# A strided convolution moved wholly onto TensorE, in 16 tiles of 32 x 32

## What is computed

```python
# 512 channels in, 256 out: each output channel has two input channels, a 3 x 3 window and stride 2
x = jax.lax.conv_general_dilated(sx, w_down, window_strides=(2, 2), padding=((1, 1), (1, 1)),
                                 feature_group_count=c2, dimension_numbers=('NCHW', 'OIHW', 'NCHW'))
# -> (8, 256, 64, 64)
labels = _kmeans_labels(xs)              # channels of image 0 into 8 clusters
v5 = ...                                 # cluster means of all images; then a small mixture fit
pre_up = gate[:, :, None, None] * x + x
up = jnp.repeat(pre_up, 2, axis=1) * w_up[None, :, None, None]
sx = _bilinear_up_x2(up) + sx            # end of layer 0
# layer 1: bias, resampling by 2 up, leaky relu, resampling by 2 down, with 12-tap filters
```

## Time and profile before

| | |
|---|---|
| median of 3 runs | 8536.89 us |
| the profiled execution | 8535.32 us |
| its span, first to last instruction | 8533.3 us |
| TensorE busy (matmuls; weight loads) | 92%; 81% |
| VectorE, ScalarE, GpSimd busy | 83%, 50%, 30% |
| granted TensorE clock, mean | 0.962 |
| DMA | 925.43 MB, mean 108 GB/s |
| convolution's work | about 37 to 1080 us |

### The profile page before, as it was taken

The page is one execution under the profiler, slowest core; times in us unless marked ns, Lnnn a source line. Parts: engine busy times, 40 slices in busy tenths (PEclk is TensorE's granted clock), DMA queues, the critical chain, the costliest instruction groups (busy, mean ns, idle before and its releaser), DMA issues.

```text
span 8533.3 us, 384310 instructions
## 1 busy us (share of the span) xinstructions
PE 7892.4 (92%) x151493; PEld 6882.4 (81%) x151493; DVE 7050.4 (83%) x12643; ACT 4274.0 (50%) x9070; POOL 2567.4 (30%) x3076
## 2 busy tenths in 40 slices
PE   7888855099999999999999999999999999999999
PEld 3444431089999999999999999999999999999999
DVE  8999933878888888888888888888888888888888
ACT  0000003356665556665556665566666556666555
POOL 0000000033333333333333333333333333333333
PEclk9999967599999999999999999999999999999999
DMA  7777713022222222222222222222222222222222
GB/s 294 297 292 292 296 61 129 0 82 84 84 84 84 84 84 84 84 84 84 84 84 84 84 84 84 84 84 84 84 84 84 84 84 84 84 84 84 84 84 81
DMA packets 1253329, 925.43 MB, mean 108 GB/s; under 512 B 175312, under 2 KB 1224912, under 8 KB 1234384
## 3 DMA queue, kind: packets, MB, share of 16 engines
q1 hardware_dynamic: 703248, 621.60, 21.5%
q10 hardware_dynamic: 550016, 303.11, 12.0%
HBM read 621.50 MB, written 303.04 MB: 108 GB/s over the span
## 4 chain that ended last, share of the span: by engine, by line
PE 80%; issue 0%; POOL 0%; DVE 0%; ACT 0%; DMA 0%; DVEq 0%; POOLq 0%
PE bank L976 37%; PE bank L965 20%; PE twin L965 15%; PE bank L970 4%; PE bank L1005 2%; PE twin L970 1%; DMA low<-conv_dram 0%; DVE leaky L1112 0%; ACT slope_t L1059 0%; POOL lift L946 0%; POOL low_f L943 0%; POOL img L931 0%; ACT res L1072 0%; DVE up L1105 0%; DVEq L810 0%
## 5 line engine op out<-in xcount | busy, mean ns | idle before, releaser
L1059 ACT ACTIVATE slope_t<-bank 128x512 f32<-128x512 f32 x4096 | 2223.2, 595 | 2263.2 <-PE bank L970 2263.2
L1112 DVE SCALAR_TENSOR_TENSOR leaky<-bank,slope_t 128x512 f32<-128x512 f32 x4096 | 2629.6, 683 | 781.4 <-ACT slope_t L1059 781.4
L970 PE MATMUL bank<-up_t,up 64*128 64x133 f32 x16384 | 2724.0, 286 | 0.0
L965 PE MATMUL bank<-up_t,up 64*128 64x133 f32 x16384 | 2672.1, 283 | 0.1
L976 PE MATMUL bank<-down_t,leaky 128*64 128x67 f32 x65536 | 2364.4, 225 | 0.7 <-DVE leaky L1112 0.5
L976 PEld LDWEIGHTS bank<-down_t,leaky 128*64 128x64 f32 x65536 | 2077.7, 137 | 259.5 <-DVE leaky L1112 1.0
L965 PEld LDWEIGHTS bank<-up_t,up 64*128 64x128 f32 x16384 | 2150.5, 187 | 52.3 <-PE bank L970 0.3
L970 PEld LDWEIGHTS bank<-up_t,up 64*128 64x128 f32 x16384 | 2147.7, 186 | 0.0
L1097 DVE SCALAR_TENSOR_TENSOR x_sum<-lift,coef,img 128x128 f32<-128x128 f32 x4096 | 1975.0, 522 | 8.8 <-POOL img L931 8.8
L931 POOL TENSOR_TENSOR img<-img,bias_all 128x512 f32<-128x512 f32 x1024 | 1089.7, 1064 | 2902.5 <-DMA img<-in_x 2902.5
L970 PE MATMUL twin<-up_t,x_sum 64*128 64x133 f32 x8192 | 1849.9, 306 | 0.0
(11 more groups left out here) (157 smaller groups left out, 3614.3 us busy)
## 6 DMA issues: line engine op xcount, KB each, us to landing
img<-in_x SPq DMA_DIRECT2D x1024, 256.0 KB, 2.8
out<-res ACTq DMA_DIRECT2D x1024, 256.0 KB, 2.2
rows_in<-in_x SPq DMA_DIRECT2D x48, 4224.0 KB, 13.9
rows_in<-in_x SPq DMA_DIRECT2D x16, 4096.0 KB, 13.7
conv_dram<-conv ACTq DMA_DIRECT2D x64, 512.0 KB, 4.1
xb<-conv_dram SPq DMA_DIRECT2D x8, 4096.0 KB, 13.4
low<-conv_dram SPq DMA_DIRECT2D x512, 64.0 KB, 2.5
xx<-conv_dram SPq DMA_DIRECT2D x2, 2048.0 KB, 10.0
```

Source lines behind the costliest of these rows:

```text
L965: return pe.matmul(acc[:, 0:UP_REACH], src, up_t[0:HALF, 0:UP_REACH], start=first, stop=False, skip_group_check=True)
L970: return pe.matmul(acc[:, UH - UP_REACH:UH], src, up_t[HALF:P, UH - UP_REACH:UH], start=first, stop=False, skip_group_check=True)
L1059: nc.scalar.activation(slope_t[i][:], u2_acc[1 - p][i][:], ACT.Copy, scale=SLOPE * GAIN).then_inc(slope_out, 1)
L1112: v.scalar_tensor_tensor(out=leaky[1 - m % 2][:, i].rearrange("p k w -> p (k w)"), in0=u2_acc[1 - m % 2][i][:], scalar=GAIN, in1=slope_t[i ...
```

## The change

All 16 output rows of a unit are made on TensorE. The array is used as 16 tiles of 32 x 32. Tile (rt, c) has as its stationary operand the diagonal of the 32 channels 32 rt to 32 rt + 31, reads those channels' partitions, and writes to PSUM partitions 32 c to 32 c + 31 of bank 4 (n % 2) + rt: the row tile chooses the channels and the bank, and the column tile chooses which four of the 16 output rows are made. So one tap is 16 matmuls of 4 x 64 = 256 columns. The result lies in PSUM as (row group c, channel within rt) on the partitions and rt over the banks; ScalarE copies four banks into `conv`, and stores it with four DMAs, one for each c, whose pieces are 1 KB (four rows of one channel).

VectorE's passes, `v_done` and `vec_step` go; `diag` shrinks to a 32-wide diagonal for each tap. TensorE's stream has no loop any more: it is written out for all 64 units. The other engines keep their loops.

```diff
-V_ROWS = 10
-T_ROWS = QR - V_ROWS
+T = 32
+NT = P // T
+T_ROWS = QR // NT
...
+    parts["eyes"] = np.tile(np.eye(T, dtype=np.float32), (NT, 1))
...
-                diag = sb("diag", [P, CB * TAPS, P])
+
+                diag = sb("diag", [P, CB * TAPS, T])
                 rows_in = [sb(f"rows_in{i}", [P, 2, IN_ROWS, W]) for i in range(2)]
-                conv = [sb(f"conv{i}", [P, QR, WO]) for i in range(2)]
+                conv = [sb(f"conv{i}", [P, NT, T_ROWS * WO]) for i in range(2)]
...
-                def conv_in(n, i, kh, kw, r0, r1):
+                def conv_in(n, i, kh, kw, rt, r0, r1):
 
                     c0 = (1, 0, 1)[kw]
-                    return rows_in[n % 2][:, i, 2 * r0 + kh:2 * (r1 - 1) + kh + 1:2, c0:c0 + 2 * (63 if kw == 0 else 64) - 1:2]
+                    return rows_in[n % 2][T * rt:T * (rt + 1), i, 2 * r0 + kh:2 * (r1 - 1) + kh + 1:2,
+                                          c0:c0 + 2 * (63 if kw == 0 else 64) - 1:2]
...
                         if wait is not None:
-
-                            sp.wait_ge(v_done, wait)
                             sp.wait_ge(t_done, wait)
...
-                    v.tensor_tensor(diag[:], ident[:, None, :].to_broadcast([P, CB * TAPS, P]),
-                                    tap_w[:].rearrange("p b t -> p (b t)")[:, :, None].to_broadcast([P, CB * TAPS, P]),
+                    v.tensor_tensor(diag[:], const("eyes")[:, None, :].to_broadcast([P, CB * TAPS, T]),
+                                    tap_w[:].rearrange("p b t -> p (b t)")[:, :, None].to_broadcast([P, CB * TAPS, T]),
                                     ALU.mult).then_inc(diag_ready, 1)
...
-                    def unit(b, n, first):
-                        cb, q = n // NQ, n % NQ
-                        v.wait_ge(in_loaded[n % 2], 16 * (n // 2 + 1) if first else (16 * (UB // 2)) * b + 16 * (n // 2 + 1))
-                        if not (first and n < 2):
-
-                            v.wait_ge(conv_stored[n % 2], 16 * (n // 2) if first else (16 * (UB // 2)) * b + 16 * (n // 2))
-                        for s, (i, kh, kw) in enumerate(order):
-                            r0 = 1 if (q == 0 and kh == 0) else 0
-                            dst = conv[n % 2][:, r0:V_ROWS, (1 if kw == 0 else 0):]
-                            w = tap_w[:, cb, (i * 3 + kh) * 3 + kw:(i * 3 + kh) * 3 + kw + 1]
-                            src = conv_in(n, i, kh, kw, r0, V_ROWS)
-                            last = s == TAPS - 1
-                            if s == 0:
-                                ins = v.tensor_scalar(dst, src, w, None, ALU.mult)
-                            else:
-
-                                v.wait_ge(vec_step, (TAPS - 1) * n + s if first else (TAPS - 1) * UB * b + ((TAPS - 1) * n + s))
-                                ins = v.scalar_tensor_tensor(out=dst, in0=src, scalar=w, in1=dst, op0=ALU.mult, op1=ALU.add)
-                            ins.then_inc(v_done if last else vec_step, 1)
-
-                    for n in range(UB):
-                        unit(0, n, True)
-                    with v.Fori(1, B) as b:
-                        for n in range(UB):
-                            unit(b, n, False)
-
                 @block.tensor
...
 
-                    def unit(b, n, first):
-                        cb = n // NQ
-                        pe.wait_ge(in_loaded[n % 2], 16 * (n // 2 + 1) if first else (16 * (UB // 2)) * b + 16 * (n // 2 + 1))
-                        if not (first and n < 2):
-
-                            pe.wait_ge(t_copied, n - 1 if first else UB * b + (n - 1))
-                        acc = bank[n % 2][:, 0:T_ROWS * WO].rearrange("p (r w) -> p r w", r=T_ROWS)
+                    def unit(b, n):
+                        cb, q = n // NQ, n % NQ
+                        g = UB * b + n
+                        pe.wait_ge(in_loaded[n % 2], 16 * (g // 2 + 1))
+                        if g >= 2:
+                            pe.wait_ge(t_copied, g - 1)
                         for s, (i, kh, kw) in enumerate(order):
-                            mm = pe.matmul(acc[:, :, (1 if kw == 0 else 0):],
-                                           diag[:, cb * TAPS + (i * 3 + kh) * 3 + kw, :],
-                                           conv_in(n, i, kh, kw, V_ROWS, QR), start=(s == 0), stop=(s == TAPS - 1),
-                                           skip_group_check=True)
+
+                            for c in range(NT):
+                                r0 = 1 if (q == 0 and c == 0 and kh == 0) else 0
+                                for rt in range(NT):
+                                    acc = bank[4 * (n % 2) + rt][T * c:T * (c + 1), 0:T_ROWS * WO].rearrange("p (r w) -> p r w", r=T_ROWS)
+                                    mm = pe.matmul(acc[:, r0:, (1 if kw == 0 else 0):],
+                                                   diag[T * rt:T * (rt + 1), cb * TAPS + (i * 3 + kh) * 3 + kw, :],
+                                                   conv_in(n, i, kh, kw, rt, T_ROWS * c + r0, T_ROWS * (c + 1)),
+                                                   start=(s == 0), stop=(s == TAPS - 1), skip_group_check=True)
                         mm.then_inc(t_done, 1)
 
-                    for n in range(UB):
-                        unit(0, n, True)
-                    with pe.Fori(1, B) as b:
+                    for b in range(B):
                         for n in range(UB):
-                            unit(b, n, False)
+                            unit(b, n)
 
                 @block.scalar
                 def _(act):
@@ -271,15 +247,17 @@
                         cb, q = n // NQ, n % NQ
                         act.wait_ge(t_done, n + 1 if first else UB * b + (n + 1))
                         if not (first and n < 2):
-                            act.wait_ge(conv_stored[n % 2], 16 * (n // 2) if first else (16 * (UB // 2)) * b + 16 * (n // 2))
-                        nc.scalar.activation(conv[n % 2][:, V_ROWS:, :].rearrange("p r w -> p (r w)"),
-                                             bank[n % 2][:, 0:T_ROWS * WO], ACT.Copy).then_inc(t_copied, 1)
+                            act.wait_ge(conv_stored[n % 2], 16 * NT * (n // 2) if first else (16 * NT * (UB // 2)) * b + 16 * NT * (n // 2))
+                        for rt in range(NT):
+                            ins = nc.scalar.activation(conv[n % 2][:, rt, :], bank[4 * (n % 2) + rt][:, 0:T_ROWS * WO], ACT.Copy)
+                        ins.then_inc(t_copied, 1)
 
                         act.wait_ge(t_copied, n + 1 if first else UB * b + (n + 1))
-                        act.wait_ge(v_done, n + 1 if first else UB * b + (n + 1))
                         rows = conv_dram[cb * P:(cb + 1) * P] if first else conv_dram[bass.ds(C * b + cb * P, P)]
-                        act.dma_start(rows[:, q * QR * WO:(q + 1) * QR * WO],
-                                      conv[n % 2][:].rearrange("p r w -> p (r w)")).then_inc(conv_stored[n % 2], 16)
+                        rows = rows.rearrange("(t c) p -> c t p", t=NT)
+                        for c in range(NT):
+                            at = (q * QR + c * T_ROWS) * WO
+                            act.dma_start(rows[:, :, at:at + T_ROWS * WO], conv[n % 2][T * c:T * (c + 1)]).then_inc(conv_stored[n % 2], 16)
 
                     for n in range(UB):
                         unit(0, n, True)
@@ -287,7 +265,7 @@
                         for n in range(UB):
                             unit(b, n, False)
                     for i in range(2):
-                        act.wait_ge(conv_stored[i], 16 * B * UB // 2)
+                        act.wait_ge(conv_stored[i], 16 * NT * B * UB // 2)
 
 
         def clusters(soh, sohn):
```

More of the change, by code:

```diff
@@ L142, in convolution @@
                 tap_w = sb("tap_w", [P, CB, TAPS])
-                diag = sb("diag", [P, CB * TAPS, P])
+                diag = sb("diag", [P, CB * TAPS, T])
                 rows_in = [sb(f"rows_in{i}", [P, 2, IN_ROWS, W]) for i in range(2)]
-                conv = [sb(f"conv{i}", [P, QR, WO]) for i in range(2)]
+                conv = [sb(f"conv{i}", [P, NT, T_ROWS * WO]) for i in range(2)]
                 in_loaded = [sem(f"in_loaded{i}") for i in range(2)]
                 conv_stored = [sem(f"conv_stored{i}") for i in range(2)]
-                vec_step = sem("vec_step")
                 diag_ready = sem("diag_ready")
-                v_done = sem("v_done")
                 t_done = sem("t_done")
```

## The result

The changed kernel takes 8902.34 us, the median of four runs (8897.23 to 8905.46), against 8536.72 before: a ratio of 1.0428, interval 1.041 to 1.0446. It is slower by 4.3%, 366 us; 8595 was forecast. The profiled execution took 8901.62 us. First the page of after: TensorE's and VectorE's slices and the granted clock, and the queue of instructions.

The account below looks back on a forecast made before the run. One DMA engine carrying data and instruction fetches was taken to bound the convolution: 37.1 us first load + 63 periods of 17.3 us (1090) + 15 = 1142 us, +60 us, forecast 8595 us; range 8250 to 9000.

Parts of the forecast that it names:

- the sum's own +60 us: Next stage's load after the convolution goes out at 1142 us instead of 1082.5, so the kernel is 60 us slower.
- VectorE sets the period before, and its passes are gone: Convolution: VectorE set the 16.3 us unit period; its taps, 952.2 us in 1088 passes, all on the path, go.
- The count of fetches: TensorE's written-out convolution: 1152 records a unit at 265 per 16 KB packet of q8 need 4.3 packets.
- It is not free for the load: Convolution loads: a fetch packet holds one DMA engine 0.94 to 1.23 us, so the load beside it lands later.
- That engine's work per unit would be 12.0 + 4.3 x 1.23 = 17.3 us: Convolution: one DMA engine carries data and all fetches and bounds the load, 17.3 us a unit; chance 0.45.
- fetches come too slowly: Rival, convolution: packets 5.5 us apart starve TensorE, 23.7 us a unit, 8999 us; chance 0.13.
- TensorE's 8.3 us a unit: Convolution matmuls: all sixteen tiles stream at once, 18 x 2 x 0.230 us = 8.3 us a unit.
- The two rivals that doubted this: Convolution: tiles don't all overlap (9598 us, chance 0.12); weight loads hold back same-row matmuls (9600 us or above, chance 0.05).
- ScalarE and its stores: Convolution: four evictions and four store issues take 3.4 us of a 17.3 us unit, beside the rest.

Follow-up runs that it names:

- the loop: The changed kernel with TensorE's unit looped, one body per block of channels, rows_in split by input channel, PSUM single: 8477.65 us, ratio 0.9932.

## Why the prediction was wrong

The sign, slower, was right and the size was not: +58 us forecast (the sum's own +60 us would make 8597, not 8595), +366 measured. As the step that was to give the sign failed, the sign is partly luck. Step by step:

- *VectorE sets the period before, and its passes are gone:* right. The beginning is the same, 37.1 and 37.2 us, and the resampling does not change: all of the difference is in the convolution.
- *The count of fetches*, 4.3 packets a unit: nearly; bursts of 128 matmuls with 128 weight loads give 4.5. 64 x 4.3 = 275 packets were forecast, and 288 came. The 265 records per packet were counted in a trace window and are 256.
- *"It is not free for the load"*: the effect exists. Loads land after 15.7 us, as in the earlier trace rows with fetches beside them, not 13.9. But it bounds nothing.
- **The step that failed** is the choice of what these fetches limit: "That engine's work per unit would be 12.0 + 4.3 x 1.23 = 17.3 us". I priced a fetch by how long its packet holds a DMA engine, 0.94 to 1.23 us, and not by how long TensorE waits from one packet to the next. That is 3.8 us without loads and 6.8 beside one: one packet at a time, most of which is not transfer (the packet at 511.48 us moves for 0.95 of 6.77 us). 4.5 packets at 4.9 us are the 22.0, and 64 x (22.0 - 16.3) = 365 us is the whole loss.
- I had that case as a rival, "fetches come too slowly", with 23.7 us a unit and 8999 us, and its break-even at 3.8 us per packet. It got 0.13, because in the earlier trace rows TensorE's demand might have set the 5.5 us between packets. That was true, and it also meant that no row bounded the fetch from above. A resource seen only when nothing presses it should have had more of the chance. The sign written down for this rival, TensorE idle with its rows landed and no semaphore to wait for, is what the trace shows. The Trainium skill (Runtime: NRT & Kernel Launch, Instruction fetch mechanics) states blocks of 256 instructions, which the bursts of 128 pairs confirm, and that dispatch is slower than the fill; here a packet's instructions ran in 2.83 us and the next came after 6.77, so for this form of matmul the trace disagrees.
- *TensorE's 8.3 us a unit:* mis-sized. In the loop a record costs 20.0 ns, not 14.4 (0.230 us over sixteen tiles), so 576 cost 11.5 us. All sixteen tiles do overlap: one alone would need 213 ns a record. The two rivals that doubted this wanted 33.2 us a unit and fall, though the 6.7 ns on top of each stream may come from the weight loads. It decided nothing here, for 11.5 us is well under the fetch's 22.0.
- *ScalarE and its stores:* hidden, though each of the four stores now lands after 11.9 us, where the one store landed after 4.1.

## What to carry to other kernels

Cutting a matmul into tiles multiplies TensorE's instructions (an fp32 matmul has four records here, two matmuls and two weight loads); count instructions per us of work and compare with the fetch, here 256 every 3.8 to 6.8 us, before counting columns. Keep such a loop's body short enough to stay resident (one of 1152 records did, one of 9216 didn't), or give each instruction more columns: 512 instead of 256 gave 8384 us written out and 8324 looped, against 8537 before and 8902 as changed. The mark of a starved engine in a profile is idle time put down to "issue", between bursts of equal length, with no semaphore late.

## What the runs showed of the hardware

- TensorE's instructions arrive in packets of 16 KB, 256 instructions, one at a time: 3.8 us each with little other traffic, 6.8 us beside a load that keeps the DMA engines full. Cutting the load's packets from 16.5 to 4 KB took the mean over the convolution only from 4.9 to 4.8 us.
- Of 6.77 us beside a load the packet itself moves for 0.95. Bursts of 1.94, 2.83 and 4.7 us are followed by the next 6.2, 6.8 and 6.5 us after they began: the fetch overlaps the burst before it.
- A loop of 1152 records and a few more instructions stays resident (27 packets in the whole run); one of 9216 is fetched again at each turn (318).
- Sixteen 32 x 32 tiles run side by side in fp32: 13.3, 20.0 and 33.6 ns per matmul record for 128, 256 and 512 columns, each with its own weight load.
